# Norm statistics and residual sum of three batches moved into attention's last groups; zero rows written from two queues

## The reference, cut to what matters

```python
x = x + _layernorm(_attn_ref(_layernorm(x)))
x = x + _layernorm(_ffn_ref(_layernorm(x)))

def _layernorm(x, eps=1e-05):
    m = mean(x, -1); v = var(x, -1)
    return (x - m) / sqrt(v + eps)

def _ffn_ref(x, Wg, gamma, beta, W1, b1, W2, b2):   # E = 8 experts, K = 2
    w, idx = top_k(x @ Wg, 2); w = softmax(w)
    xhat = (x - mean(x)) * rsqrt(var(x) + 1e-6)
    normed = xhat * gamma[e] + beta[e]
    out = relu(normed @ W1[e] + b1[e]) @ W2[e] + b2[e] + x
    return sum of w * out over the token's two experts
```

## Time and profile before

| what | value |
|---|---|
| median of three runs | 1284.81 us |
| the profiled execution's own time | 1284.04 us |
| its span, first to last instruction | 1282.4 us |
| TensorE busy | 1053.0 us, 82% |
| VectorE busy | 823.3 us, 64% |
| ScalarE busy | 640.8 us, 50% |
| GpSimd busy | 576.7 us, 45% |
| mean granted TensorE clock | 0.896 |

### The profile page before, as it was taken

The page is one execution under the profiler, slowest core; times in us unless marked ns, Lnnn a source line. Parts: engine busy times, 40 slices in busy tenths (PEclk is TensorE's granted clock), DMA queues, the critical chain, the costliest instruction groups (busy, mean ns, idle before and its releaser), DMA issues. The chain is left out here.

```text
span 1282.4 us, 24075 instructions
## 1 busy us (share of the span) xinstructions
PE 1053.0 (82%) x7325; PEld 805.8 (63%) x7325; DVE 823.3 (64%) x2492; ACT 640.8 (50%) x1109; POOL 576.7 (45%) x671
## 2 busy tenths in 40 slices
PE   5979999999999999998533603999999999999900
PEld 2535555555555555554233503999999999999900
DVE  5738887777777777773188521556655655565577
ACT  2640566666666666666444412444444444454533
POOL 4202455655655555556747771223222222232237
PEclk9995999999999999999855555999999999999955
DMA  4993344455544545453261245142441414421173
GB/s 133 371 351 110 133 131 143 169 173 172 170 149 175 159 159 159 162 170 118 88 244 66 79 145 189 54 161 64 182 176 50 176 50 177 148 78 50 41 270 131
DMA packets 93837, 189.99 MB, mean 148 GB/s; under 512 B 27476, under 2 KB 58596, under 8 KB 85500
## 3 DMA queue, kind: packets, MB, share of 16 engines
q1 hardware_dynamic: 84496, 165.10, 37.4%
q0 software_dynamic: 7680, 22.09, 5.0%
q10 hardware_dynamic: 1588, 1.92, 0.5%
HBM read 109.50 MB, written 79.05 MB: 147 GB/s over the span
## 5 line engine op out<-in xcount | busy, mean ns | idle before, releaser
L772 ACT ACTIVATE att_pt<-att_ps_s 128x1024 f32<-128x1024 f32 (+3 forms) x384 | 298.0, 814 | 181.1 <-PE att_ps_s L694 177.6
L796 DVE CUSTOM_DVE_ANT_0 att_ps_m<-att_ps_m,keep_future 128x384 f32<-128x384 f32 (+2 forms) x384 | 204.0, 584 | 67.2 <-PE att_ps_m L657 67.0
L1504 ACT ACTIVATE moe_hf<-moe_ps_h,moe_b 128x256 f32<-128x256 f32 x288 | 134.3, 474 | 225.7 <-PE moe_ps_h L1460 211.1
L805 DVE TENSOR_REDUCE att_pm<-att_ps_m 128x1 f32<-128x512 f32 x256 | 161.2, 683 | 25.9 <-PE att_ps_m L657 25.8
L614 POOL TENSOR_SCALAR_AFFINE_SELECT att_pt<-att_pt 128x512 f32<-128x512 f32 x128 | 81.3, 635 | 184.4 <-ACT att_pt L772 184.4
L1413 POOL DMA_INDIRECT ys<-moe_o,moe_home x72 | 74.2, 1030 | 186.9 <-DVE moe_o L1543 173.6
L657 PE MATMUL att_ps_m<-att_k,att_q 128*128 128x512 f32 (+2 forms) x480 | 150.9, 385 | 3.5 <-DVE att_pm L796 2.1
L694 PE MATMUL att_ps_s<-att_q,att_k 128*128 128x512 f32 (+1 forms) x480 | 129.6, 357 | 3.4 <-ACT att_pt L772 2.5
L1537 DVE TENSOR_TENSOR moe_hTl<-moe_hf,moe_hTh 128x256 fp32r<-128x256 f32 x288 | 123.9, 430 | 10.0 <-DVE moe_hTh L1535 0.2
L604 POOL TENSOR_TENSOR att_rec<-att_sums,att_minus 128x16 f32<-128x16 f32 x32 | 93.0, 2906 | 39.3 <-ACT att_sums L761 39.3
L657 PEld LDWEIGHTS att_ps_m<-att_k,att_q 128*128 128x128 f32 x480 | 82.5, 193 | 42.8 <-issue 13.1
(11 more groups left out here) (197 smaller groups left out, 2585.0 us busy)
## 6 DMA issues: line engine op xcount, KB each, us to landing
att_raw<-in_w SPq DMA_DIRECT2D x16, 1024.0 KB, 5.5
ws<-att_raw_hi SPq DMA_DIRECT2D x16, 1024.0 KB, 4.0
ws<-att_raw SPq DMA_DIRECT2D x16, 1024.0 KB, 6.0
moe_rows<-xs SPq DMA_DIRECT2D x38, 258.0 KB
weights_w_0h<-ws SPq DMA_DIRECT2D x8, 1024.0 KB
weights_w_0l<-ws SPq DMA_DIRECT2D x8, 1024.0 KB
att_q<-qs SPq DMA_DIRECT2D x27, 256.0 KB
att_k<-ks SPq DMA_DIRECT2D x54, 128.0 KB
```

The costliest lines, as they stand in the source:

```text
L772: act.activation(pt[:, blk % NPT, 2 * p:2 * p + 2, off:CH], ps_s[k % 2][:, :, off:CH], ACT.Exp, scale=HS ** -0.5).then_inc(ex_done, 1)
L796: ins = dve.tensor_tensor_reduce(part, part, future[:, CH - keys:CH], 1.0, LOWEST, ALU.add, ALU.max, pm[:, g % 2, 0, head, place:place + 1])
L805: return dve.tensor_reduce(pm[:, g % 2, 0, h, place:place + 1], src, AX.X, ALU.max)
L1504: act.activation(hf[:, f % NHB], ps_h[f % NHB][:], ACT.Relu, bias=b1[r][:, f:f + 1]).then_inc(hf_done, 1)
```

## The change

In `attend`, a 3 MB load of x is issued in group 13 (`gone` = 13). The moments of y of batches 0, 1 and 2 are made on VectorE in steps 0 to 15 of groups 12, 13 and 14, one instruction to a step, their roots on GpSimd in steps (13, 10), (14, 10) and (14, 16). After its last unit VectorE makes `early_sum` of the three batches: norm, sum with x, moments of the sum. GpSimd takes the roots of those in steps (15, 9) and (15, 13) and after the last divide. The second and third norm share their moments: with v and m of x1, the factor of xf is (v + 1e-5)^-0.5 and that of xh is (v (1 + 1e-6) + 1e-5 * 1e-6)^-0.5, so xb, its moments and its copy are gone, and ScalarE makes xf and xh from x1. In `route` the loops are written out for all four batches, only batch 3 has moments, roots, norm_y and residual left, and the zero rows are written four from SyncE's queue, four from ScalarE's.

```diff
+PRE = 3
+def roots_of_heads(pool, keep, b, n, aggregated, prepared, rooted, known):
+    pool.wait_ge(aggregated, n * TB + TB)
+    pool.tensor_scalar(veps[:, b, 0], mv[:, 0, b, :, 1], LN_EPS, None, ALU.add).then_inc(prepared, 1)
+    pool.tensor_scalar(nmean[:, b, 0], mv[:, 0, b, :, 0], -1.0, None, ALU.mult).then_inc(prepared, 1)
+    pool.wait_ge(prepared, n * 2 + 2)
+    pool.tensor_tensor(rstd[:, b, 0], veps[:, b, 0], keep["mhalf"][:, 0], ALU.pow).then_inc(rooted, 1)
+    pool.wait_ge(rooted, n + 1)
+    pool.tensor_tensor(keep["shift"][:, b, 0], nmean[:, b, 0], rstd[:, b, 0], ALU.mult).then_inc(known, 1)
+def roots_of_sums(pool, keep, b, n, aggregated, prepared, rooted, known):
+    pool.wait_ge(aggregated, n * TB + TB)
+    pool.tensor_scalar(veps[:, b, 1], mv[:, 1, b, :, 1], LN_EPS, None, ALU.add).then_inc(prepared, 1)
+    pool.tensor_scalar(veps[:, b, 2], mv[:, 1, b, :, 1], 1.0 + MOE_EPS, LN_EPS * MOE_EPS, ALU.mult, ALU.add
+                       ).then_inc(prepared, 1)
+    pool.tensor_scalar(nmean[:, b, 1], mv[:, 1, b, :, 0], -1.0, None, ALU.mult).then_inc(prepared, 1)
+    pool.wait_ge(prepared, n * 3 + 3)
+    pool.tensor_tensor(rstd[:, b, 1:3], veps[:, b, 1:3], keep["mhalf"][:], ALU.pow).then_inc(rooted, 1)
+    pool.wait_ge(rooted, n + 1)
+    pool.tensor_tensor(keep["shift"][:, b, 1:3], nmean[:, b, 1:2].to_broadcast([P, 2, TB]), rstd[:, b, 1:3], ALU.mult
+                       ).then_inc(known, 1)
...
+        gone = GROUPS - 3
+        HEAD_ROOTS = ((gone, 10), (gone + 1, 10), (gone + 1, 16))[:PRE]
+        SUM_ROOTS = ((GROUPS - 1, 9), (GROUPS - 1, 13))
...
@@ attend, sync
                         load_group(sp, d, slots, g + 2)
+                    if g == gone:
+                        sp.dma_start(early_x[:], d["x"][0:PRE * T, :].rearrange("(k p) c -> p k c", p=P)).then_inc(x_in, 16)
                     if g + 1 < GROUPS:
                         max_rows(g + 1)
@@ attend, gpsimd
                                 divide(g, what[2], n)
+                        if (g, k) in HEAD_ROOTS:
+                            b = HEAD_ROOTS.index((g, k))
+                            pool.wait_ge(halves, 1)
+                            roots_of_heads(pool, keep, b, b, y_aggr, y_ve, y_root, y_rs)
+                        if (g, k) in SUM_ROOTS:
+                            b = SUM_ROOTS.index((g, k))
+                            roots_of_sums(pool, keep, b, b, x_aggr, x_ve, x_root, x_rs)
                 divide(GROUPS, 0, LAST[1])
+                roots_of_sums(pool, keep, 2, 2, x_aggr, x_ve, x_root, x_rs)
@@ attend, vector
+                def head_moments(b, k):
+                    if k < TB:
+                        dve.bn_stats(stats[:, 0, b, k], head_tile(keep, b, k)).then_inc(y_stat, 1)
+                        return
+                    if k == TB:
+                        dve.wait_ge(y_stat, b * TB + TB)
+                    if k < 2 * TB:
+                        dve.bn_aggr(mv[:, 0, b, k - TB], stats[:, 0, b, k - TB]).then_inc(y_aggr, 1)
+                def early_sum(b):
+                    dve.wait_ge(y_rs, b + 1)
+                    for t in range(TB):
+                        dve.tensor_scalar(head_tile(keep, b, t), head_tile(keep, b, t), mv[:, 0, b, t, 0:1],
+                                          rstd[:, b, 0, t:t + 1], ALU.subtract, ALU.mult).then_inc(yn_done, 1)
+                    dve.wait_ge(yn_done, b * TB + TB)
+                    for t in range(TB):
+                        dve.tensor_tensor(head_tile(keep, b, t), head_tile(keep, b, t),
+                                          early_x[:, b * TB + t].rearrange("p (g w) -> p g w", g=NG), ALU.add
+                                          ).then_inc(x1_done, 1)
...
                 jobs(FIRST)
-                for steps in DEAL:
-                    for step in steps:
+                for g, steps in enumerate(DEAL):
+                    b = g - gone + 1
+                    if b in range(PRE):
+                        dve.wait_ge(y_done, 2 * (b + 1) * NG)
+                    for k, step in enumerate(steps):
                         jobs(step.all())
+                        if b in range(PRE):
+                            head_moments(b, k)
+                dve.wait_ge(x_in, 16)
+                for b in range(PRE):
+                    early_sum(b)
...
@@ route
+        def pad_rows(eng, experts):
+            eng.wait_ge(consts, 4)
+            eng.wait_ge(homes, 2)
+            eng.wait_ge(pad_known, 1)
+            settle(eng, keep["passed"])
+            for e in experts:
+                row = eng.value_load(pad[0:1, e:e + 1], min_val=e * CAP, max_val=e * CAP + N)
+                eng.dma_start(d["xs"][bass.ds(row, XT), :].rearrange("(k p) c -> p k c", p=P),
+                              zeros[:]).then_inc(padded, 16)
...
-                for b in range(B):
+                for b in range(PRE, B):
                     sp.dma_start(xf[:, b * TB:(b + 1) * TB], d["x"][b * T:(b + 1) * T, :].rearrange("(k p) c -> p k c", p=P)
...
+                pad_rows(sp, range(E // 2))
@@ route, gpsimd
-                cuts = (0, 5, 10, K * TB)
...
+                for b in range(PRE, B):
+                    roots_y(b)
+                for b in range(B):
+                    scatter(b, 0, K * TB // 2)
+                    if b + PRE < B:
+                        roots_x(b + PRE)
+                    scatter(b, K * TB // 2, K * TB)
@@ route, vector
+                for b in range(PRE, B):
+                    moments(b, 0, y_stat, y_aggr)
...
+                for b in range(B):
+                    pick_experts(b)
+                    if b + PRE < B:
+                        residual(b + PRE)
@@ route, scalar
+                def norm_x(b):
+                    if b >= PRE:
+                        act.wait_ge(x_rs, b - PRE + 1)
+                        settle(act, keep["passed"])
                     for t in range(TB):
+                        act.activation(by_group(xf, b * TB + t), head_tile(keep, b, t), ACT.Identity, scale=rstd[:, b, 1, t:t + 1],
+                                       bias=shift[:, b, 1, t:t + 1]).then_inc(xf_done, 1)
+                        if t > 0:
+                            keep_turned(b, t - 1)
+                    keep_turned(b, TB - 1)
                     for t in range(TB):
+                        ins = act.activation(by_group(xh[:, :, 0:C], b * TB + t), head_tile(keep, b, t), ACT.Identity,
+                                             scale=rstd[:, b, 2, t:t + 1], bias=shift[:, b, 2, t:t + 1])
                     ins.then_inc(xh_done, 1)
...
+                for b in range(B):
+                    norm_x(b)
+                    if b + PRE < B:
+                        norm_y(b + PRE)
                 act.wait_ge(weights_in, 1)
                 act.activation(wgt[:, 1], de[:], ACT.Exp).then_inc(exp_done, 1)
+                pad_rows(act, range(E // 2, E))
@@ route, tensor
-                with pe.Fori(0, B) as b:
+                for b in range(B):
...
-                                ins = pe.transpose(ps_x[t % 2][:, k], xb[:, t, k * P:(k + 1) * P], ident[:])
+                                ins = pe.transpose(ps_x[t % 2][:, k], tile(xf, b, t)[:, k * P:(k + 1) * P], ident[:])
```

159 lines of the change are left out of this document (56 added, 103 removed).

## The result

| | before | after |
|---|---|---|
| median (12 runs each, same chip) | 1285.04 us | 1278.62 us |
| the profiled execution's own time | 1284.04 us | 1276.48 us |
| its span | 1282.4 us | 1274.8 us |

The ratio is 0.9947, 95% interval 0.9933 to 0.9961: faster by 6.4 us where 13.8 were forecast (1271 against 1284.81). The time lies inside the range. One of the twelve executions of after took 1781.95 us at a granted clock of 0.554, and the ratio leaves it out.

What follows compares the result with a forecast made beforehand. TensorE was taken to bound attend and the experts, GpSimd to bound route. Route gives back 37.5 us, attend's end moves 24.1 later: -13.4 from 1284.04 is 1270.6, stated as 1271, range 1257 to 1283.

Steps and rivals of the forecast that it cites:

- Part 3: Route's end: zero rows covered by scatters, second queue worth 0; 3 us behind last scatter, route 110, giving back 37.5.
- Part 1: Route's chain before the scatters: first scatter 21.5 us into route instead of 40.5.
- Part 2: Route's scatters: 64 at 1.27 us with one roots call of 4.3 between, last issued at 107; later batches ready early.
- Rival C: Route gives back less: code fetching makes batches late and GpSimd wait; 1286, or likelier 1278; chance 0.12.
- Part 4: Group 14 of attend: two heads' roots calls on GpSimd delay the clears of blocks 8 and 9; +3.5 us.
- Part 7: Groups 12 to 14 of attend: VectorE's moments make TensorE wait for banks, 1 us a group; +3 us.
- Part 5: Group 15 of attend: two sums' roots calls on GpSimd between split and divide; +8.3 us.
- Part 8: TensorE's clock falls around the stops: +1.5 us early in group 15, +2.5 for last value products; +4 us.
- Part 6: Attend's end: a third sums' roots call alone on the path after the last divide; +4.3 us.
- Part 9: Attend's port and queue: early load 0; GpSimd beside VectorE's adds +1 us, or 5 by the skill's whole-train blocking view.
- Rival A: Attend hides GpSimd's additions in group 14 and TensorE's clock stays: 1260 us or less; chance 0.13.
- Rival B: TensorE's clock falls in groups 14 and 15 and does not come back: slower, 1296 us; chance 0.07.

Runs made afterwards that it cites:

- run 1: The changed kernel unchanged, on another chip than the result's; 1292.12 us, ratio to before 1.0039, route 126.7 us.
- run 13: The kernel before with all the change's new buffers and semaphores allocated and unused; 1287.42 us, ratio to before 1.0036.
- run 16: The kernel before with only the change's seven small buffers allocated ahead of the others, unused; 1289.18 us, ratio to before 1.0034.
- run 2: The changed kernel with all eight zero rows written from SyncE's queue; 1290.27 us, against 1292.12 for the unchanged changed kernel beside it.
- run 5: The kernel before, unchanged, traced beside changed kernels on another chip; 1285.9 us (one run), route 148.1 us.
- run 12: The kernel before, unchanged, traced on a further chip; 1282.51 us (one run), route 148.2 us.
- Run 3: The changed kernel with the three sums' roots moved from attend to route's start; 1275.58 us, against 1292.12 for the changed kernel beside it.
- run 8: The changed kernel with sums' roots moved into route and heads' moments and roots one group earlier; 1259.5 us, against 1276.89 for the changed kernel.
- run 11: The same version as run 8 (both moves) on another chip; 1256.87 us, against 1277.36 for the changed kernel beside it.

## Why the prediction was wrong, and where it was right

The direction and the mechanism held; the gain was forecast at 13.4 and was 7.6 by the traces. Of the 5.8 missing, 3.6 are attend's and 2.7 route's, and the experts gave back 0.5. That the time fell inside the range owes something to the chip: in run 1 the same kernel took 1292.12, outside it. Two steps failed.

- **Part 3, the end of route.** "3 us for it and the Block's end", between 2 and 4.5; it is 8.15 from the last scatter's start. The landing was sized well (2.4), but the Block's end had next to nothing in the sum, and GpSimd's drain there takes 5.28. That is 5.15 us too little. Luck gave 2.1 back, since the last scatter came at 104.9 instead of 107 (1.4 of it from the first scatter, the rest mostly because 64 scatters have 63 steps between them); so route is 113.05 instead of 110, against 147.84 in before, and 2.7 of the gain are gone. A row that was at hand shows the tail: the last scatter at 774.29 and the experts' load at 782.43 are 8.1 apart.
- **A cost with no part at all.** Before group 12 nothing was put; 5.1 us were lost in the traced pair, 4.5 in the mean of all traces, 3.5 without the one step that differs from execution to execution in every kernel. Runs 13 and 16 show that buffers which move the others cost 2.7 and 4.8 us by themselves. The forecast priced instructions only, not the room they need.

The rest, step by step:

- **Part 1**: first scatter 21.5 forecast, 20.1 measured.
- **Part 2**: last scatter 107, measured 104.9; one `roots` between, 5.71 from scatter to scatter instead of 1.27, so 4.4 where 4.3 were forecast. Batches ready ahead of their scatters: right on the chip of the result (the 64 run without another stop), wrong on two of five, see Rival C.
- **Part 3, zero rows**: 0 for the second queue, right by run 2. The 3.9 us for one row was a price of that trace; runs 5, 12 and 13 issue all eight in 9.2.
- **Part 4 and Part 7 in group 14**: forecast 3.5 + 1, measured 11.8 - 6.8 = 5.0, of which 4.16 are the stop for GpSimd's clear.
- **Part 5 with most of Part 8**: forecast 8.3 + 2.5, measured 21.8 - 11.8 = 10.0, a stop of 8.54 and 1.5 of lower clock (Part 8). Run 3 confirms the size, run 8 that it goes away.
- **Part 6**: 4.3; the third call runs from 657.8 to 662.0.
- **Part 7 in groups 12 and 13**: forecast 2, measured 1.7 (the lag grows from 5.1 to 6.8). TensorE is still the bound there, with 30.75 of 31.8 us busy.
- **Part 8, the clock**: it did fall after both stops, to 0.59 in the 3.8 us behind the first and over the 22 at the end, and it was back at 1.00 between them. What it cost can be read from the 16 value products behind each stop: 3.19 us instead of 1.70, 1.5 each time. The first 1.5 lies in the 10.0 above, the second in the remainder at attend's end, 27.7 - 5.1 - 1.7 - 5.0 - 10.0 - 4.3 = 1.6. Together 3 where 4 was put.
- **Part 9**: no row shows a cost of the early load (DMA share 0.78 in group 13, issued at 558.2). GpSimd beside VectorE's trains: a product of 0.21 us took 0.46 at 602.76, a power of 2.91 took 3.08 at 603.19, and with the other small losses it is some 1 us in all, as put. A train that blocks GpSimd for its whole length, the 5 us of the other view, is not seen. VectorE's own trains were slowed more, below, without a wait behind them.

Without the loss before group 12, attend's parts come to 22.6 where 24.1 were put.

**Rival A** did not happen: both stops are there in full. **Rival B** did not: the clock came back in group 15. **Rival C** did, on two of five chips: one late batch after another, 14 us of the gain gone (126.7 against 113.1), and then the change is 0.4% slower than before. The forecast's "against", 14 us of work against 20 of scatters, was right on average and did not ask what one batch 22 us late would do once the cover was thinner: before had its batch 3 up to 7 late with no effect. Its cause, code fetched for written-out loops, is not shown by anything here; the late turns in the first trace of before, where TensorE's loop is not written out, speak against it as the whole cause.

## What to carry to other kernels

Ask of each piece that is moved not how long it takes but where its engine has slack: the same 13 us of GpSimd work cost 13.4 or more at a point where TensorE waited for GpSimd's next instruction, and 1.0 where GpSimd itself was waiting for the first places. A tail is read from the last event of its own queue to the next stage, not from whichever transfer ends near it, and what lies in it is looked up: here it was less the landing than the drain behind it. And new buffers allocated ahead of old ones move the old ones: time the old kernel with the new buffers unused before believing a sum of instructions to 5 us.

## What the runs showed of the hardware that was not expected

- Unused buffers, 3520 bytes per partition ahead of the others, made the kernel 0.34% slower (interval 0.21 to 0.47).
- The DRAIN with which GpSimd leaves a Block that ends in indirect DMAs takes 5.28 or 5.29 us in all traces, after the last transfer has landed (2.4 us from its start in after); at attend's end, behind a GpSimd product, it takes 0.33 to 0.73. What it waits for is not shown.
- On two of five chips completions of matmuls come up to 15.0 us late, in the same two batches in six kernels; the traces that show it lack many semaphore counts.
- One kernel, two executions: before the 16 value products of block 8 in group 14 TensorE stood still 1.38 us in run 11 and 1.42 in run 8. The granted clock over the products was 1.00 in run 11, which took 1.70 us for them, and 0.50 (1.2 GHz) in run 8, which took 3.19.
- VectorE's tensor_scalar train beside GpSimd. The Trainium skill (SBUF — State Buffer, section "Who interferes with whom") says that tensor_scalar can contend with GpSimd when it runs in one of the modes that use two ports. No run here tells in which mode these ran. Eight instructions with one tensor input, and two scalars per partition, took 5.74 us while GpSimd ran the split and 3.60 and 3.32 at the two other places, against 2.64 for eight of them in before's route; that agrees with such a contention. VectorE after, first two batches:

```profile
596.63 5.74 DVE L906 TENSOR_SCALAR keep_y<-keep_y,keep_mv,keep_rstd 128x256 f32<-128x256 f32 x8
602.40 2.81 DVE L910 TENSOR_TENSOR keep_y<-keep_y,att_early_x 128x256 f32<-128x256 f32 x8
...
608.55 3.60 DVE L906 TENSOR_SCALAR keep_y<-keep_y,keep_mv,keep_rstd 128x256 f32<-128x256 f32 x8
```
